# Reordering the first two groups of a fused cross-attention and expert kernel

## The chip, the cores and the metric

The kernel runs on one core of a Trainium2 chip. The metric is the device time of one execution, in microseconds (us). The engines are TensorE (PE, with its weight loads PEld), VectorE (DVE), ScalarE (ACT), GpSimd (POOL) and SyncE (SP), which issues most DMA transfers; ACT and POOL can issue transfers as well.

## The reference

One layer of a gated cross-attention block, with 16 sequences of 128 tokens and 256 channels, all in fp32. Cut to what matters:

```python
x = x + tanh(g_xattn) * attention(layernorm(x), ctx, mask, Wq, Wkv)   # 16 heads of 16 channels
x = x + tanh(g_ffn) * ffn(layernorm(x))                               # top 2 of 8 experts, and a shared FFN
# attention, per sequence:
q = layernorm(x) @ Wq.T;  k, v = split(ctx @ Wkv.T)                   # ctx: 128 rows of 192 channels
p = softmax(where(mask, (q * d ** -0.5) @ k.T, -1e9))                 # per head, over the 128 keys
out = p @ v
```

The change concerns the attention of the first four sequences alone.

## The kernel before

The 16 sequences are handled as 8 groups of two (256 tokens each). For each group g the kernel computes keys, queries and values on TensorE, the scores of each head, the softmax, the value product, the residual and the second norm, and then the router. The experts and the shared FFN follow after the groups.

**Per group.** For each half of the queries (j) and each half of the heads (h): `scores(g, j, h)` on PE (line 1422), `maxima(g, j, h)` on DVE (line 959), then per j `pieces` (line 965), a transpose `max_t` (line 1440 on PE, line 667 on ACT), the copy `max_rows`, `scores_t(g, j, h)` (line 1456), `exp` on ACT (line 673), the value product `values` (line 1473), a copy and a transpose (`heads_out`, `values_t`), and on DVE the division, the residual and the statistics of the second norm.

**Order.** Each engine runs one hand-written list, with semaphore waits. Behind an opening for groups 0 and 1 stands a loop over s from 2, which works on several groups at once: in step s the scores of group s-2, the queries of group s-1 and the keys of group s. The wait of an instruction holds everything behind it on its engine. The opening stands in the lists as follows.

- SP (line 406 on): loads of x in three parts (2, 2 and 12 blocks; the last is line 414, 1536 KB), context, weights; then the copies of group 0.
- POOL (line 561): powers for the first norm (`power1`), the memset of the ones rows, the third pieces of groups 0 and 1.
- ACT (line 722): `norm1(0)` (first norm of two blocks), `normed_t(0)` (its transpose out of PSUM), `norm1(1)`, and only then the pieces of group 0.
- DVE (line 1090): statistics and norms of blocks 0 to 3, the differences of group 0, statistics of the last 12 blocks (`stats(4, B)`, line 1101), the difference of group 1's keys, the last norms, four small conversions (line 1104).
- PE (line 1592): 56 warming products, the gates' product, 24 warming products, the transposes `normed_t(0)`, keys, queries, then group 1's keys and the values, `scores(0, 0, 0)`, `scores(0, 0, 1)`; the queries of group 1 open step s = 2 (line 1622), and `scores(1, 0, 0)` stands behind `scores_t(0, 0, 1)` (line 1666).

The functions that the diff touches:

## Time and profile before

| what | value |
|---|---|
| median of 3 runs | 333.09 us (332.68 to 334.06) |
| span of the profiled execution | 329.2 us |
| the profiled execution's own time | the profile gives its span alone; the median of the runs is 3.9 us above that |
| TensorE busy | 304.6 us (93%) |
| VectorE busy | 243.6 us (74%) |
| ScalarE busy | 169.2 us (51%) |
| GpSimd busy | 129.8 us (39%) |
| chain that ended last | PE 41%, DVE 18%, issue 17%, POOL 8%, DMA 7%, SP queue 5% |

The span runs from the first to the last instruction of the program. Busy shares are averages over stages that differ; the opening, the first 36 us or so, is a stage of its own, in which transfers are short of room and the engines wait for each other. The chain of waits is followed back from the last instruction, at each step to what released it. In a timeline row the columns are start, length, engine, line, operation, tile written and tiles read, shapes, count, and in brackets the idle time ahead of it and what ended it. SPq and ACTq are the issue of a transfer by that engine, not the transfer.

### The profile page before, as it was taken

Reading aid. Unit: us, or ns where it says so; the run is one execution under the profiler, and the core shown is the slowest. Engines: PE = TensorE matmul, PEld = TensorE weight load, DVE = VectorE, ACT = ScalarE, POOL = GpSimd, SP = SyncE. Lnnn points to the kernel's source line nnn. Section 1 sums busy time; section 2 is a strip of 40 time slices with the busy share of each in tenths; the row PEclk is TensorE's granted clock in tenths of the full one; section 3 lists DMA queues with packets and bytes.
Section 4 is the critical chain, followed back from the end, with each engine's and each line's share of the span. In section 5 each row is a group of like instructions: output and inputs, shape, how many; then the busy total and the mean of one; then the engine's idle time right before and its main releaser. Section 6 shows DMA issues by size and latency. Waiting matters only on the chain.

```text
span 329.2 us, 8082 instructions
## 1 busy us (share of the span) xinstructions
PE 304.6 (93%) x2505; PEld 244.5 (74%) x2505; DVE 243.6 (74%) x728; ACT 169.2 (51%) x322; POOL 129.8 (39%) x151
## 2 busy tenths in 40 slices
PE   7948889999989979998999989999999999999986
PEld 7627667787768755655465758889988898888875
DVE  4576597798999998687679976666666666633895
ACT  2444767777777744365495236444454444424131
POOL 5732143232465744506760085744333433331000
PEclk9998999999999999996999999999999999999999
DMA  7882776586666362166226112333333333103941
GB/s 232 255 217 80 227 197 207 161 263 193 189 186 177 123 178 84 50 201 250 98 98 164 44 34 83 106 94 108 94 103 98 97 85 111 64 16 133 416 153 64
DMA packets 34069, 47.18 MB, mean 143 GB/s; under 512 B 5519, under 2 KB 27667, under 8 KB 33522
## 3 DMA queue, kind: packets, MB, share of 16 engines
q1 hardware_dynamic: 28706, 34.61, 35.3%
q0 software_dynamic: 4320, 10.92, 9.9%
q10 hardware_dynamic: 1008, 1.18, 1.2%
q8 instruction: 22, 0.36, 0.5%
q14 instruction: 13, 0.11, 0.1%
HBM read 22.20 MB, written 12.62 MB: 106 GB/s over the span
## 4 chain that ended last, share of the span: by engine, by line
PE 41%; DVE 18%; issue 17%; POOL 8%; DMA 7%; SPq 5%; ACT 2%; POOLq 0%; DVEq 0%
PE ps L1744 27%; POOL dispatched L541 4%; DMA stacks<-work 4%; DVE x_all L1334 3%; DVE fc_lo L1177 3%; SPq L381 3%; PE ps L1790 3%; PE ps L1716 2%; PE ps L1562 2%; POOL rs L526 2%; PE ps L1437 1%; SPq L374 1%; DVE fc_lo L1183 1%; DMA stacks<-expert_rows 1%; PE ps L1407 1%
## 5 line engine op out<-in xcount | busy, mean ns | idle before, releaser
L597 POOL DMA_INDIRECT expert_rows<-v_s,slot_u x39 | 38.3, 982 | 58.6 <-ACT v_s L867 46.3
L963 DVE TENSOR_REDUCE mx<-ps 128x8 f32<-128x1024 f32 x32 | 39.1, 1223 | 13.0 <-PE ps L1437 12.7
L1284 DVE TENSOR_TENSOR act<-ps,sil 128x256 f32<-128x256 f32 x39 | 16.6, 425 | 29.9 <-ACT sil L860 29.8
L549 POOL TENSOR_TENSOR work<-work 128x512 bf16<-128x512 f32 x16 | 18.5, 1156 | 50.3 <-ACT work L646 50.2
L677 ACT ACTIVATE probs<-ps 128x1024 f32<-128x1024 f32 x32 | 32.7, 1022 | 9.4 <-PE ps L1470 9.4
L860 ACT ACTIVATE sil<-ps 128x256 f32<-128x256 f32 x39 | 15.0, 384 | 41.4 <-PE ps L1744 41.3
L1744 PE MATMUL ps<-fc_hi,xs_hi 128*128 x78 | 34.2, 439 | 1.4 <-DVE xs_lo L1265 1.4
L1744 PE MATMUL ps<-fc_hi,xs_lo 128*128 x78 | 30.7, 394 | 0.0
L1744 PE MATMUL ps<-fc_lo,xs_hi 128*128 x78 | 30.7, 394 | 0.0
L867 ACT ACTIVATE v_s<-ps,wt 128x256 f32<-128x256 f32 x39 | 18.5, 475 | 19.0 <-PE ps L1744 19.0
L1437 PE MATMUL ps<-stacks 96*128 96x128 bf16 x256 | 20.1, 222 | 7.0 <-DVE mx L963 3.3
L1437 PEld LDWEIGHTS ps<-stacks 96*128 96x128 bf16 x256 | 16.0, 100 | 10.3 <-DVE mx L963 4.8
L1744 PE MATMUL ps<-fc_hi,act_hi 128*128 x78 | 22.1, 283 | 0.2 <-DVE act_lo L1295 0.2
L1744 PE MATMUL ps<-fc_lo,act_hi 128*128 x78 | 22.0, 282 | 0.0
L1744 PE MATMUL ps<-fc_hi,act_lo 128*128 x78 | 21.9, 281 | 0.0
L1470 PEld LDWEIGHTS ps<-stacks 99*128 99x128 bf16 x256 | 15.8, 98 | 6.9 <-issue 5.4
L1470 PE MATMUL ps<-stacks 99*128 99x128 bf16 x256 | 19.7, 220 | 0.5 <-ACT probs L677 0.5
L1486 PE MATMUL ps<-probs,v_s 128*32 128x128 f32 x512 | 18.6, 281 | 1.1 <-DVE att L985 0.8
L1293 DVE CAST act_hi<-ps 128x256 fp32r<-128x256 f32 x39 | 16.5, 423 | 3.2 <-PE ps L1790 3.2
L541 POOL DMA_INDIRECT dispatched<-row_s,slot_u x16 | 16.0, 1000 | 7.4 <-issue 4.1
L1295 DVE TENSOR_TENSOR act_lo<-ps,act_hi 128x256 fp32r<-128x256 f32 x39 | 16.6, 424 | 1.3
L526 POOL TENSOR_TENSOR rs<-ve,mhalf 128x1 f32<-128x1 f32 x16 | 9.1, 566 | 21.4 <-DVE ve L996 21.4
(221 smaller groups left out, 828.4 us busy)
## 6 DMA issues: line engine op xcount, KB each, us to landing
stacks<-work SPq DMA_DIRECT2D x75, 128.0 KB, 3.1
xs_in<-dispatched SPq DMA_DIRECT2D x39, 129.0 KB, 2.0
fc_s<-in_fc SPq DMA_DIRECT2D x8, 512.0 KB, 5.2
stacks<-work POOLq DMA_DIRECT2D x18, 128.0 KB, 3.4
ctx_s<-in_ctx_t SPq DMA_DIRECT2D x8, 256.0 KB, 3.7
fc_s<-in_fc SPq DMA_DIRECT2D x8, 256.0 KB, 5.3
stacks<-expert_rows SPq DMA_DIRECT2D x2, 1024.0 KB, 5.8
probs<-expert_rows SPq DMA_DIRECT2D x2, 1024.0 KB, 9.9
```

Of the source, the lines that this page charges most:

```text
L541: nc.gpsimd.indirect_dma_start(xs, bass.IndirectOffsetOnAxis(slot_u[:, g, m:m + 1], 0), rows_of[g][:, m, :], None, bounds_check=NULL_ROW + ...
L549: nc.gpsimd.tensor_tensor(out[:, 2, :], rest, out[:, 1, :], ALU.subtract).then_inc(ready, 1)
L597: nc.gpsimd.indirect_dma_start(ys, bass.IndirectOffsetOnAxis(dst_u[:, r:r + 1], 0), y_out[:, r, :], None, bounds_check=2 * T - 1, oob_is_e ...
L677: nc.scalar.activation(probs[:, 2 * j + h], ps_t, ACT.Exp, scale=HD ** -0.5).then_inc(probs_ok[j][h], 1)
L867: nc.scalar.activation(y_out[:, r, :], ps[:, 5 + r % 2, 0:D], ACT.Copy, scale=wt[:, r:r + 1]).then_inc(y_ok, 1)
L963: nc.vector.reduce_max(mx[:, j, 8 * h:8 * h + 8], ps_s, AX_X).then_inc(max_ok[j][h], 1)
L1284: nc.vector.tensor_tensor(act[:, par], ps[:, 2 + par, FI:2 * FI], sil[:, par], ALU.mult).then_inc(act_ok, 1)
L1295: nc.vector.tensor_tensor(act_lo[:, par], whole, act_hi[:, par].bitcast(F32), ALU.subtract).then_inc(actt_ok, 1)
L1437: last = nc.tensor.matmul(ps_s[:, n, :], q_st[at], k_st[at], start=True, stop=True)
L1470: last = nc.tensor.matmul(ps_t[:, n, :], k_st[at], q_st[at], start=True, stop=True)
L1486: last = nc.tensor.matmul(ps_o[row:row + VW, blk:blk + P], v_s[:, g % 2, j, VW * head:VW * head + VW], probs[:, 2 * j + h, n, :], start=Tr ...
L1744: ins = nc.tensor.matmul(out, a, b, start=first and n == 0, stop=last and n == 2)
```

## The change

In words:

- PE computes the keys of group 0 ahead of the transposes of its rows, and runs 12 warming products behind the transposes instead of 24 ahead of them. The queries of group 1 move up between `scores(0, 0, 0)` and `scores(0, 0, 1)`. `scores(1, 0, 0)` stands ahead of `scores_t(0, 0, 1)`.
- ACT cuts the first key piece behind `norm1(0)`, the second one behind `normed_t(0)`, and only then runs `norm1(1)`. Its two copies of the first query piece are issued each behind a piece; the third copy goes to SP. The query pieces and the values of group 1 move up from step 3 to step 2, ahead of `norm1(2)`.
- DVE takes the key difference of group 0 ahead of the norm of blocks 2 and 3. The norm of the last 12 blocks and group 1's query difference stand between the first two maxima. The small conversions move to the end of step 2.
- POOL fills the ones rows behind the third pieces of group 0, with a wait on the third query piece instead of the one on the powers.
- SP issues the copies of group 1's first key piece ahead of the load of group 2's context, and group 1's query copies in step 2, with the row of maxima between the second and the third piece.

```diff
             stack_k(0, 0)
             stack_k(0, 1)
             stack_k(0, 2)
+            sp.wait_ge(q_ok[0], 1)
+            sp.dma_start(q_st[5:PIECES * HD:PIECES, 0].rearrange("p h t -> p (h t)"),
+                         q_pc[:, 0, :]).then_inc(qst[0], 16)
             stack_q(0, 1)
             stack_q(0, 2)
+            stack_k(1, 0)
 
             for s in range(2, G + 3):
-                if live(s - 3):
+                if live(s - 3) and s > 3:
                     max_rows(s - 3, 0)
-                if live(s - 2) and s > 2:
+                if live(s - 2) and s > 3:
                     stack_q(s - 2, 0)
                     stack_q(s - 2, 1)
                     stack_q(s - 2, 2)
...
                     load_shared(s - 3)
                 if live(s - 1):
                     stack_free(s - 1)
-                    stack_k(s - 1, 0)
+                    if s > 2:
+                        stack_k(s - 1, 0)
                     stack_k(s - 1, 1)
                     stack_k(s - 1, 2)
+                if s == 2:
+                    stack_q(1, 0)
+                    stack_q(1, 1)
+                    max_rows(0, 0)
+                    stack_q(1, 2)
 
             for e in range(EARLY, E):
                 load_first(e)
...
 
             power1(0, 2, 1)
             power1(2, 4, 2)
-            pool.wait_ge(rs1_ok, 2)
+            third(0, kst, k_rest, k_ok[1], k_pc, k_ok[2])
+            third(0, qst, q_rest, q_ok[1], q_pc, q_ok[2])
+            pool.wait_ge(q_ok[2], 1)
             nc.gpsimd.memset(k_f[PIECES * HD:PIECES * HD + 3, :], TWO_ONES).then_inc(kones_ok, 1)
             pool.wait_ge(kones_ok, 1)
-            third(0, kst, k_rest, k_ok[1], k_pc, k_ok[2])
-            third(0, qst, q_rest, q_ok[1], q_pc, q_ok[2])
             power1(4, B, 3)
             third(1, kst, k_rest, k_ok[1], k_pc, k_ok[2])
             third(1, qst, q_rest, q_ok[1], q_pc, q_ok[2])
...
 
             sa.wait_ge(gates_done, 1)
             nc.scalar.activation(tg[:, :], ps_c[:, 0:2], ACT.Tanh).then_inc(tanh_ok, 1)
+            def copy_of_q(row):
+
+                sa.wait_ge(q_ok[0], 1)
+                sa.dma_start(q_st[row:PIECES * HD:PIECES, 0].rearrange("p h t -> p (h t)"),
+                             q_pc[:, 0, :]).then_inc(qst[0], 16)
+
             norm1(0)
+            first(0, k_done, kst, k_pc, k_ok[0])
             normed_t(0)
+            second(0, kr_ok, k_rest, k_pc, k_ok[1])
             norm1(1)
-            first(0, k_done, kst, k_pc, k_ok[0])
-            second(0, kr_ok, k_rest, k_pc, k_ok[1])
             first(0, q_done, qst, q_pc, q_ok[0], ps_q0)
+            copy_of_q(0)
             second(0, qr_ok, q_rest, q_pc, q_ok[1])
-            sa.wait_ge(q_ok[0], 1)
-            for p, row in Q_ROWS:
-                if p == 0:
-                    sa.dma_start(q_st[row:PIECES * HD:PIECES, 0].rearrange("p h t -> p (h t)"),
-                                 q_pc[:, p, :]).then_inc(qst[0], 16)
+            copy_of_q(3)
             values_in(0)
             normed_t(1)
             for s in range(2, G + 2):
...
                     exp(s - 4, 1, 1)
                 if live(s - 5):
                     tokens_t(s - 5)
-                if live(s - 2) and s > 2:
+                if live(s - 2) and s > 3:
                     first(s - 2, q_done, qst, q_pc, q_ok[0])
                 if live(s - 3):
                     max_t(s - 3, 0)
-                if live(s - 2) and s > 2:
+                if live(s - 2) and s > 3:
                     values_in(s - 2)
                     second(s - 2, qr_ok, q_rest, q_pc, q_ok[1])
                 if live(s - 5):
...
                     max_t(s - 3, 1)
                 if live(s - 1):
                     first(s - 1, k_done, kst, k_pc, k_ok[0])
-                if s == 2:
-                    norm1(s)
                 if live(s - 3):
                     exp(s - 3, 0, 1)
                 if s == G + 1:
...
                     exp(s - 3, 1, 0)
                 if live(s - 1):
                     second(s - 1, kr_ok, k_rest, k_pc, k_ok[1])
+                if s == 2:
+                    first(1, q_done, qst, q_pc, q_ok[0])
+                    values_in(1)
+                    second(1, qr_ok, q_rest, q_pc, q_ok[1])
+                    norm1(s)
                 if live(s - 5):
                     second_score(s - 5)
                     second_row(s - 5, 1)
...
             first_norm(0, 2, 1)
             ve.wait_ge(x_in1, 16)
             stats(2, 4)
+            rest(0, ps_kq, k_ok[0], k_pc, k_ok[2], k_rest, kr_ok)
             first_norm(2, 4, 2)
-            rest(0, ps_kq, k_ok[0], k_pc, k_ok[2], k_rest, kr_ok)
             rest(0, ps_q0, q_ok[0], q_pc, q_ok[2], q_rest, qr_ok)
             ve.wait_ge(x_rest, 16)
             stats(4, B)
             rest(1, ps_kq, k_ok[0], k_pc, k_ok[2], k_rest, kr_ok)
-            first_norm(4, B, 3)
-            ve.wait_ge(const_ok, 11)
-            nc.vector.tensor_copy(e_f[:, :], e_i[:, :]).then_inc(dve_link, 1)
-            nc.vector.tensor_copy(t_f[:, :], t_i[:, :]).then_inc(dve_link, 1)
-            links[0] += 2
-            link(nc.vector.tensor_copy(dest_f[:, :], dest_i[:, :]))
-            link(nc.vector.tensor_scalar(er_f[:, :], e_f[:, :], float(R), None, ALU.mult))
+            def numbers():
+
+                ve.wait_ge(const_ok, 11)
+                nc.vector.tensor_copy(e_f[:, :], e_i[:, :]).then_inc(dve_link, 1)
+                nc.vector.tensor_copy(t_f[:, :], t_i[:, :]).then_inc(dve_link, 1)
+                links[0] += 2
+                link(nc.vector.tensor_copy(dest_f[:, :], dest_i[:, :]))
+                link(nc.vector.tensor_scalar(er_f[:, :], e_f[:, :], float(R), None, ALU.mult))
+
             relink()
             for s in range(2, G + 2):
                 if live(s - 2):
                     maxima(s - 2, 0, 0)
+                if s == 2:
+                    first_norm(4, B, 3)
+                    rest(1, ps_kq, q_ok[0], q_pc, q_ok[2], q_rest, qr_ok)
                 if live(s - 1) and s > 2:
                     rest(s - 1, ps_kq, k_ok[0], k_pc, k_ok[2], k_rest, kr_ok)
                 if live(s - 4):
...
                     residual(s - 3, 0)
                 if live(s - 2):
                     maxima(s - 2, 1, 0)
-                if live(s - 1):
+                if live(s - 1) and s > 2:
                     rest(s - 1, ps_kq, q_ok[0], q_pc, q_ok[2], q_rest, qr_ok)
                 if live(s - 5):
                     weights(s - 5)
...
                     logits(s - 4)
                 if live(s - 2):
                     pieces(s - 2, 1)
+                if s == 2:
+                    numbers()
                 if s == G + 1:
                     times_0(1)
                 if live(s - 4):
...
             pe.wait_ge(small_in, 32)
             pe.wait_ge(const_ok, 11)
             nc.tensor.matmul(ps_c[:, 0:2], ones_r[:, :], gate_r[:, :], start=True, stop=True).then_inc(gates_done, 1)
-            warm(24)
-            normed_t(0)
             keys_main(0)
             for c in range(2):
                 keys_rest(0, c)
+            normed_t(0)
+            warm(12)
             queries(0)
             keys_main(1)
             values_main(0)
...
             for j in range(2):
                 values_rest(1, j)
             scores(0, 0, 0)
+            queries(1)
             scores(0, 0, 1)
             for s in range(2, G + 2):
-                if live(s - 1):
+                if live(s - 1) and s > 2:
                     queries(s - 1)
                 if live(s - 2):
                     scores(s - 2, 1, 0)
...
                     for c in range(2):
                         keys_rest(s, c)
                         values_rest(s, c)
+                if s == 2:
+                    scores(1, 0, 0)
                 if s == G:
                     shared_0(2)
                     shared_0(3)
...
                     shared_0(10)
                 if live(s - 2):
                     scores_t(s - 2, 0, 1)
-                if live(s - 1):
+                if live(s - 1) and s > 2:
                     scores(s - 1, 0, 0)
                 if live(s - 4):
                     positions(s - 4)
```

## Rows read from the trace of the kernel before

**Rows 1.** Chain of waits, 0 to 80 us: start, length, what.

```profile
18.63 4.08 DMA stacks<-work
...
33.69 2.40 DMA stacks<-work
...
50.28 0.62 PE ps L1437 x8
```

**Rows 2.** Timeline of ACT, 6 to 50 us.

```profile
10.61 1.09 ACT L633 ACTIVATE work<-x_all,nm,rm 128x256 f32<-128x256 f32 x2 [0.85 <-DVE nm L936]
11.61 0.57 ACT L642 ACTIVATE work<-ps 128x512 bf16<-128x512 f32 x1
...
35.53 1.02 ACT L677 ACTIVATE probs<-ps 128x1024 f32<-128x1024 f32 x1
```

**Rows 3.** Timeline of PE, 6 to 42 us.

```profile
6.71 1.51 PE L1597 MATMUL ps<-ones_b 128*128 128x128 bf16 x24
...
9.92 1.13 PE L1378 MATMUL ps<-ctx_s,wk_s 64*128 64x256 f32 x4
...
22.75 0.62 PE L1437 MATMUL ps<-stacks 96*128 96x128 bf16 x8 [1.44 <-DMA stacks<-work]
24.69 1.03 PE L1437 MATMUL ps<-stacks 96*128 96x128 bf16 x8 [1.32 <-DVE mx L963]
25.52 3.12 PE L1407 MATMUL ps<-work,wq_s 128*128 128x256 f32 x8
...
30.41 0.62 PE L1437 MATMUL ps<-stacks 96*128 96x128 bf16 x8 [1.15 <-DVE mx L963]
...
34.87 0.62 PE L1470 MATMUL ps<-stacks 99*128 99x128 bf16 x8
36.13 0.62 PE L1437 MATMUL ps<-stacks 96*128 96x128 bf16 x8 [0.64 <-DMA stacks<-work]
36.69 1.08 PE L1486 MATMUL ps<-probs,v_s 128*32 128x128 f32 x32
...
39.89 1.95 PE L1407 MATMUL ps<-work,wq_s 128*128 128x256 f32 x8
```

**Rows 4.** Timeline of SP's transfer issues, 5 to 36 us.

```profile
5.19 0.48 SPq L414 DMA_DIRECT2D x_all<-in_x  x1
12.21 5.07 SPq L374 DMA_DIRECT2D stacks<-work  x6
...
30.48 3.81 SPq L381 DMA_DIRECT2D stacks<-work  x6
```

**Rows 5.** DMA issue at 5.1 to 5.2 us: KB, us from issue to landing.

```profile
x_all<-in_x SPq DMA_DIRECT2D x1, 1536.0 KB, 8.5
```

**Rows 6.** Busy time by stretch, then granted clock, DMA share, GB/s.

```profile
16.10:21.90 5.80, 2.84 (x12) 1.76 (x12) 4.03 (x22) 1.88 (x3) 2.54 (x2) 1.00 1.04 245
```

**Rows 7.** Timeline of DVE, 4 to 34 us.

```profile
14.69 4.01 DVE L924 BATCH_NORM_STATS2 st<-x_all 128x6 f32<-128x256 f32 x12
...
21.56 0.69 DVE L957 TENSOR_TENSOR work<-ps,work 128x512 f32<-128x512 f32 x1 [1.71 <-ACT work L642]
...
23.41 1.23 DVE L963 TENSOR_REDUCE mx<-ps 128x8 f32<-128x1024 f32 x1 [0.37 <-PE ps L1437]
...
27.51 0.17 DVE L971 TENSOR_SCALAR mx_pc<-mx 128x16 bf16<-128x16 f32 x1 [0.52 <-DVE mx L963]
```

**Rows 8.** Timeline of POOL, 9 to 28 us.

```profile
10.24 3.51 POOL L564 MEMSET stacks<- 3x4096 f32 x1
13.83 1.16 POOL L549 TENSOR_TENSOR work<-work 128x512 bf16<-128x512 f32 x1
...
19.93 2.27 POOL L522 TENSOR_TENSOR rs<-ve,mhalf 128x12 f32<-128x12 f32 x1 [3.26 <-DVE ve L931]
```

**Rows 9.** Busy time by stretch, then granted clock (third from the end), DMA share, GB/s.

```profile
24.50:27.90 3.40, 3.21 (x14) 2.76 (x15) 1.71 (x4) 0.00 (x0) 0.99 (x1) 0.50 0.46 126
...
150.80:157.60 6.80, 6.09 (x25) 3.11 (x26) 4.53 (x22) 3.65 (x7) 5.00 (x6) 0.50 0.51 195
```

## Prediction

> **What bounds the kernel now.** I read the chain of waits first, over the opening 80 us. It ties the opening to the copies that build the stacks: the last copy of group 0 is issued at 18.63 and takes 4.08 us, and the last one of group 1 ends just as TensorE begins that group's scores, at 36.13; group 2's begin at 50.28 [rows 1]. From 36.13 on the groups follow in steps of 14.15 us, each released by the one before, and the loads of later weights are issued inside these steps. What the opening gains or loses is therefore handed on to the end; nothing in the chain is held to a fixed time.
>
> The timelines of the engines come next, then the DMA issues. Group 0's first key copy is late for a reason of order: ScalarE normalizes group 1's rows (10.61, 1.09 us) before it cuts the first key piece at 11.61 [rows 2], although the key product ends at 11.05 and TensorE could have run it sooner: it stands behind the second warming series (6.71, 1.51 us) and the transposes [rows 3]. The load of the remaining rows of x, 1536 KB, is issued at 5.19 on SP and lands 8.5 us later, at 13.7 [rows 4, 5]. After that the DMA engines are far from full until 16.1, and then full to 21.9, at 245 GB/s [rows 6]. The hole between the two is what can be had.
>
> **The opening, part by part.** The key product goes ahead of the transposes and of 12 warming products, which replace 24; it needs only transfers that the wait for the gates outlasts. It starts at about 6.8, takes two halves of some 1.1 us [rows 3], and the piece (0.57) is cut by 9.6, ahead of the transposed rows and of group 1's normalization [rows 2]. SP then issues three copies from 9.6 instead of 12.21 [rows 4]. They gain less than these 2.6 us: on SP's queue they sit behind the 1536 KB, whose data end near 12.9, if landing takes the 0.8 us that lie between the end of the full stretch and the first scores (21.9 to 22.7) [rows 3, 5, 6]. The copy of the transposed rows follows the key piece, to 10.2, and the query product (1.95, [rows 3]) ends at 12.2.
>
> Query pieces: first 0.57, difference 0.69, second about 0.6, third 1.16 [rows 2, 7, 8]; with hops of 0.04 the third is ready at 15.4. The last copy is issued then, not at 18.63. ScalarE now issues two copies between its pieces instead of three behind them; at SP's price, 0.64 each (six in 3.81, [rows 4]), the second difference covers the first, and the values' product the other. The third is SP's own.
>
> **When are the twelve copies in?** Two sums. By data: 12 x 131 KB at 245 GB/s is 6.4 us after 12.9, and 0.8 to land: 20.1 [rows 6]. By issue: 15.4, 0.6 for the issue ahead of it, and the 4.08 us of [rows 1]: 20.1. Some loss between the queues added, I take 20.45 against 22.75: **-2.3**. The ends: if the data ran as fast as they could, group 1's first key difference on VectorE would hold the gain to about 3.0 (below). At the late end, SP's first six issues took 5.07 us instead of 3.8 [rows 4]; 1.2 more gives 21.5, a gain of 1.2.
>
> **The ones rows.** The memset (3.51 us, [rows 8]) moves behind both third pieces and a new wait on the query piece. Queued behind it on POOL are the power of the last twelve blocks and group 1's third pieces; VectorE's second norms wait for the power. The memset would run 15.4 to 18.9. The power needs the statistics of the rest of x, which now start at 14.69 and let the power go at 19.93, 5.2 us later [rows 7, 8]; started at 13.7 they end at 18.9. So the memset costs nothing; were this cover gone, each us past 18.9 would first use up the 1.2 us until VectorE asks for the power's result. The removed wait, on the first two powers, held nothing up. SP's new wait, on a piece whose successor it awaits next, costs its one copy.
>
> **Group 1, and what the new order makes wait.** Its first key piece must wait until all six key copies have landed, about 17.9 at the forecast's rate; the difference then waits for VectorE's statistics, to 18.9, and takes 0.69: 19.6, against 22.25 now [rows 7]. Group 1's query product now stands between the two halves of the first scores on TensorE, and its difference between the two maxima on VectorE. Added up from the start of the first scores: 0.5 of scores, 1.95 product, 0.57 piece, 0.69 difference, 1.23 maximum, 1.3 for the pieces of the maxima (idle 0.52, then 0.8 of four small instructions), 1.23 maximum, 0.25 of hops: 7.72 us to the start of scores (0,1,1). Before, it is 22.75 to 30.41, 7.66 [rows 2, 3, 7]. **+0.1**: the wait that VectorE gets is paid for by the product that no longer holds up the second block's scores.
>
> From there TensorE is nearly full in both. To the second half of group 0's transposed scores it is 30.41 to 34.87, 4.46. Before, group 1's scores follow, which wait for their copies, and the values from 36.69 to 37.77, in all 7.36. Now the scores of group 1 come first: 4.46 + 0.56 + 0.62 + exponential 1.02 + half the values 0.54 + hops 0.15 = 7.35 [rows 2, 3]. **0.0**: the stall on the copies goes, and the exponential that was hidden in it comes out. Group 1's query copies: five issues of 0.64 from about 24, the row of maxima, then the last one at about 28 [rows 4]; with the 2.40 us of [rows 1] it lands near 30.4, and TensorE asks at 32.6. The row of maxima is wanted by 29.8 and issued at about 27; its way to landing shows in no row, so between nothing and a full copy's 2.40 of delay, and as it is much smaller than a copy I take no delay. VectorE's four small conversions (0.5) move into its idle time behind the second pieces; group 2's context is loaded behind three more issues, 1.9 us, and is wanted some 4 us after it lands.
>
> Sum: -2.3 + 0.1 + 0.0 = **-2.2 us** at an equal clock.
>
> **The clock.** TensorE's granted clock is half from 24.5 to 27.9 [rows 9]. It fell after TensorE had paused twice, 1.44 and 1.32 us, for the copies and for a maximum, with 0.62 of work between. The query product in that stretch took 3.12 instead of 1.95 [rows 3]: +1.17, which lies within the 7.66. The new order has a thin stretch too, 23.5 to 28.2, with two groups of scores in it, so a half stretch probably comes behind it, over work that TensorE does without a pause. Bounds: 0, if it ends as the full work begins; 1.7, half of its 3.4 us. I take the middle, **+0.85**.
>
> The Trainium skill, TensorE: Matmul & The Clock Gate, Part 1, calls half the clock the idle state, brought back by an idle stretch and lifted by activity; read so, the pauses here, some 2 us at most, would not bring it back, and the sum would be -2.2. The trace disagrees: the clock fell after pauses of 1.44 and 1.32 us.
>
> **Time.** The profiled execution has a span of 329.2; the median of the runs, 333.09, is 3.9 above it, which I take as what lies around the span, unchanged. -2.2 + 0.85 is -1.35: 331.7. A measurement of this kernel tells about 0.5% from no change, 1.7 us, so faster begins under 331.4.
>
> **Rivals.** One: no half stretch hits full work. For it: the new opening leaves TensorE fewer long pauses before 23. Against: [rows 9]. It gives -2.2: 330.9. It is also what the page's rule gives.
>
> Two: the copies come little earlier, because SP or the queue is late, -1.2 in place of -2.3. For it: SP's slow issues [rows 4], and key copies that wait behind x whenever they are issued [rows 5]. Against: the hole before 16.1. -1.2 + 0.1 + 0.85: 332.8.
>
> Three, the slower side: two half stretches. The first is brought by the pause before the first scores (19 to 20.4) and hits group 1's query product as it does today, +1.17; the second hits the full work, +1.7. It decides once the two cost over 2.2 together: -2.2 + 2.87 = +0.67, 333.8. For it: from 150.8 to 157.6 the clock stays at half for 6.8 us on end [rows 9]. Against: the steps from 36.13 on show none.
>
> **Chances.** Forecast 0.50 (its own range 330.9 to 332.6), one 0.24, two 0.14, three 0.12. Under 331.4 lie one's 0.24, two fifths of the forecast, 0.20, and 0.02 of two: faster 0.46. Over 334.8 lie the upper tail of three, 0.05, and 0.06 for a wait that I have not seen: slower 0.11. The rest, 0.43, is the same. The range takes in the early end of the copies without a half stretch (-2.9: 330.2), rival two and most of three: 330.2 to 333.6.
>
> **What would show it.** First key copy issued near 9.6 and landed after 14; scores of group 0 at 20.0 to 21.0; the power right behind the memset near 18.9; group 1's query product between the first two groups of scores; scores (0,1,1) near 28.2; scores of group 1 near 32.6, not released by a DMA; steps of 14.15 us afterwards. The forecast is wrong if the copies land past 21.5, if TensorE waits for group 1's copies with the transposed scores queued behind, if the power starts past 20, or if the lead at group 2's scores is gone by the end.

## Result and profile after

The changed kernel takes 335.39 us (median of 20 runs, 333.38 to 339.10), the kernel before 333.84 (20 runs, 330.64 to 335.31): a ratio of 1.0059, 95% interval 1.0036 to 1.0082. It is slower by about 2 us, 0.6%, by the ratio (1.6 us by the medians), where 1.4 us less had been forecast. A second set gave 1.0050 (1.0017 to 1.0082). A ratio leaves out runs over 1.5% above the fastest of their kernel; where a kernel's runs spread with the granted clock, ratio and medians can differ, so below the medians of all runs stand first.

The profile shown of the changed kernel is of its fastest run, 333.38 us, with a span of 331.6. So 1.8 us lie around the span, here and, within 0.1, in every run of these two kernels that lists both. The prediction had taken 3.9.

ScalarE of the changed kernel, timeline (against [rows 2]); then its transfer issues on SP ([rows 4]), and the load of x ([rows 5]):

```profile
9.12 0.60 ACT L652 ACTIVATE work<-ps 128x512 bf16<-128x512 f32 x1 [0.72 <-PE ps L1401]
...
12.39 0.60 ACT L652 ACTIVATE work<-ps 128x512 bf16<-128x512 f32 x1 [0.30 <-PE ps L1430]
```

```profile
9.74 3.89 SPq L374 DMA_DIRECT2D stacks<-work  x6
13.68 0.60 SPq L419 DMA_DIRECT2D stacks<-work  x1
14.40 2.45 SPq L381 DMA_DIRECT2D stacks<-work  x3
...
24.25 3.20 SPq L381 DMA_DIRECT2D stacks<-work  x5
28.16 0.84 SPq L403 DMA_DIRECT2D stacks<-mx_t  x1
```

```profile
x_all<-in_x SPq DMA_DIRECT2D x1, 1536.0 KB, 9.7
```

The first pieces come as worked out: keys at 9.12, queries at 12.39, first key copy issued at 9.74. But x now takes 9.7 us to land instead of 8.5. The chain of waits has group 0's last copy ([rows 1]) issued at 15.64, three us earlier than before, and longer on its way:

```profile
15.64 5.47 DMA stacks<-work
```

VectorE and GpSimd, timelines ([rows 7, 8]):

```profile
14.93 4.02 DVE L940 BATCH_NORM_STATS2 st<-x_all 128x6 f32<-128x256 f32 x12 [1.22 <-DMA x_all<-in_x]
...
22.95 0.71 DVE L951 TENSOR_TENSOR rm<-rs,mask_f 128x12 f32<-128x12 f32 x1
...
26.15 0.69 DVE L987 TENSOR_SCALAR mx_pc<-mx 128x16 bf16<-128x16 f32 x1
```

```profile
15.66 3.51 POOL L576 MEMSET stacks<- 3x4096 f32 x1
20.24 2.27 POOL L532 TENSOR_TENSOR rs<-ve,mhalf 128x12 f32<-128x12 f32 x1 [1.08 <-DVE ve L947]
22.48 1.15 POOL L559 TENSOR_TENSOR work<-work 128x512 bf16<-128x512 f32 x1
25.65 1.15 POOL L559 TENSOR_TENSOR work<-work 128x512 bf16<-128x512 f32 x1 [2.02 <-ACT work L656]
```

The statistics start 1.2 us later than forecast (14.93, not 13.7), by as much as x lands later, and the power waits for them, not for the memset. TensorE ([rows 3]):

```profile
21.15 0.62 PE L1460 MATMUL ps<-stacks 96*128 96x128 bf16 x8 [1.67 <-DMA stacks<-work]
21.61 1.95 PE L1430 MATMUL ps<-work,wq_s 128*128 128x256 f32 x8
23.39 0.61 PE L1460 MATMUL ps<-stacks 96*128 96x128 bf16 x8
26.10 1.00 PE L1460 MATMUL ps<-stacks 96*128 96x128 bf16 x8 [2.10 <-DVE mx L979]
...
28.66 1.03 PE L1460 MATMUL ps<-stacks 96*128 96x128 bf16 x8 [0.84 <-DVE mx L979]
29.49 1.06 PE L1441 MATMUL ps<-ident,work 128*128 128x128 f32 x4
30.35 1.91 PE L1396 MATMUL ps<-ctx_s,wk_s 128*128 128x256 f32 x4
...
35.20 0.62 PE L1460 MATMUL ps<-stacks 96*128 96x128 bf16 x8
35.66 0.61 PE L1493 MATMUL ps<-stacks 99*128 99x128 bf16 x8
36.20 0.64 PE L1509 MATMUL ps<-probs,v_s 128*32 128x128 f32 x16
37.39 0.65 PE L1509 MATMUL ps<-probs,v_s 128*32 128x128 f32 x16 [0.54 <-ACT probs L687]
```

The first scores start 1.60 us earlier (21.15 against 22.75), scores (0,1,1) 1.75 earlier (28.66 against 30.41), and group 1's scores (35.20) no longer wait for a copy. Then the lead goes: 0.93 is left at group 1's scores, behind work at half clock, the second half of the values waits 0.54 for an exponential, and group 2's scores start at 50.47, 0.18 later than before. Group 7's first ones are 1.66 later (126.8 before). Twice in the opening a small VectorE instruction takes 0.7 us instead of 0.17, until GpSimd's third piece beside it ends (26.15 + 0.69 and 25.65 + 1.15).

Three stretches (clock third from the end):

```profile
18.70:36.90 18.20, 13.12 (x106) 10.03 (x104) 11.48 (x35) 8.34 (x15) 5.01 (x4) 0.81 0.43 114
116.00:136.00 20.00, 17.25 (x179) 11.31 (x177) 17.80 (x50) 9.72 (x17) 7.96 (x10) 1.00 0.37 108
150.00:162.00 12.00, 10.12 (x64) 5.92 (x63) 7.91 (x32) 4.88 (x9) 8.14 (x9) 0.72 0.56 205
```

Every clock record is at one of the two levels, full or half, so the time at half in a stretch is twice its length times what the mean lacks to 1: here 6.9 us in the opening, where the profile before has 3.4 [rows 9], none about 120, 6.7 about 152 in both.

### The profile page after: what moved, and what is told of

Read it like the earlier page. It is cut to its first block, busy times and chain, and to the rows that moved or that the text cites. A ratio compares the mean times of both kernels' runs of the same rounds, so it can differ in the third digit from the quotient of the medians.

```text
span 331.6 us, 8058 instructions
## 1 busy us (share of the span) xinstructions
PE 306.0 (92%) x2493; PEld 245.4 (74%) x2493; DVE 245.3 (74%) x728; ACT 169.5 (51%) x322; POOL 129.8 (39%) x151
## 4 chain that ended last, share of the span: by engine, by line
PE 45%; DVE 18%; issue 17%; POOL 9%; DMA 6%; ACT 2%; SPq 2%; POOLq 0%; DVEq 0%
PE ps L1770 27%; POOL dispatched L551 4%; DMA stacks<-work 3%; DVE x_all L1357 3%; DVE fc_lo L1200 3%; PE ps L1816 3%; PE ps L1742 2%; PE ps L1620 2%; PE ps L1430 2%; PE ps L1585 2%; SPq L381 2%; POOL work L559 2%; DMA stacks<-expert_rows 1%; POOL rs L536 1%; PE ps L1460 1%
## 5 line engine op out<-in xcount | busy, mean ns | idle before, releaser
L1770 PE MATMUL ps<-fc_hi,act_hi 128*128 x78 | 22.3, 286 | 0.2 <-DVE act_lo L1318 0.2
L1493 PE MATMUL ps<-stacks 99*128 99x128 bf16 x256 | 20.1, 222 | 0.5 <-ACT probs L687 0.5
```

The lines of the kernel that those rows point to most:

```text
L1493: last = nc.tensor.matmul(ps_t[:, n, :], k_st[at], q_st[at], start=True, stop=True)
L1770: ins = nc.tensor.matmul(out, a, b, start=first and n == 0, stop=last and n == 2)
```

## Experiments

A table further on brings the profiles together. Where an expectation speaks of group 0's values product at 38.2 us, the mark is the scores right behind it, (1,0,1). "Warming products" are more of the 128x128 products that the kernel begins with, into a bank that nobody reads at that time; they change no result.

**1. The clock of the opening.** Both kernels get warming products in front of the waits at which TensorE paused:

```diff
+            def fill(count):
+                for n in range(count):
+                    nc.tensor.matmul(ps[:, 4, 0:P], ones_b[:, :], ones_b[:, :], start=True, stop=True)
...
+            fill(22)
             scores(0, 0, 0)
```

(a_fill: 14, 8, 22, 34 and 14 of them, ahead of `normed_t(1)`, `values_main(1)`, `scores(0,0,0)`, `scores(0,1,0)` and `scores(0,1,1)`; b_fill: 26, 8, 22, 18, 14, the fourth ahead of `scores(0,0,1)`.)

> Fills TensorE's pauses of the opening in the changed kernel with warming products into a free bank (14, 8, 22, 34, 14 of them), so that the clock has no reason to fall before 33 us. Clock theory (the change wins 1.6 us at the first scores and loses more to a longer half stretch): 1.0 to 2.5 us under the kernel before, 3 to 4 under the changed one, granted clock 0.98 or more. Order theory (group 1's queries between the first scores, and its scores ahead of the transposed ones, cost the time): still 0.5 to 2 us over the kernel before. Theory of a loss further down: lead of 1.5 us or more at group 2's scores in the trace, but not at the end of the span.

> The same filling of the pauses in the kernel before (26, 8, 22, 18, 14 products). Clock theory: about 1.2 us under the kernel before, the price of the one half stretch there, and 1 to 2 us slower than the changed kernel with its pauses filled. Order theory: also about 1.2 under, but faster than the changed kernel filled.

Measured: a_fill 333.49 us (12 runs), ratio 1.0032 (0.9991 to 1.0073); b_fill 332.96 (12 runs), 0.9989 (0.9958 to 1.0019); the kernel before on the same chip 333.95. Neither profile falls to half before 119 us. So the opening's falls come from the pauses, and filling them takes 1.9 us off the changed kernel's median (335.39 in the first set) and 1.0 off the one before. a_fill's median is 0.5 below the kernel before, where the clock theory had 1.0 to 2.5 below and the order theory 0.5 to 2 above: neither range is met. With the opening's clock equal the changed order is not the faster one. a_fill leads at the first scores by 1.4 us, and has 0.69 left at group 1's second scores, where b_fill is 1.12 ahead of the profile before without any earlier copy.

**2. Parts of the change, without warming products.** g0_only keeps group 0's part (keys first, memset and copies moved) and puts group 1's queries, rests and scores back; s100_back is the changed kernel with one line moved:

```diff
-                if s == 2:
-                    scores(1, 0, 0)
...
                 if live(s - 2):
                     scores_t(s - 2, 0, 1)
-                if live(s - 1) and s > 2:
+                if live(s - 1):
                     scores(s - 1, 0, 0)
```

> The part of the change for group 0 alone (keys first, ones rows behind the pieces, copies behind their pieces); group 1's queries, copies, norms and scores stand where they stood. Clock theory: first scores at 21.1 as with the whole change, half the loss of clock, time within 1 us of the kernel before. Order theory: 1.0 to 1.6 us under the kernel before, since the lead of the copies stays and nothing is interleaved.

> The changed kernel with group 1's first scores back behind the second half of group 0's transposed scores. Clock theory: within 0.4 us of the changed kernel (335.4 beside 333.8 of the kernel before). Order theory: 0.6 to 1.0 us faster than the changed kernel, since the exponential no longer comes out from under those scores.

Measured: g0_only 334.23 us (12 runs), ratio 1.0023 (0.9992 to 1.0053); s100_back 335.57 (12 runs), 1.0058 (1.0018 to 1.0098). g0_only starts the first scores 0.95 earlier (at 21.80, not the 21.1 expected) and has nothing of it left at 28.5 us; it is within 1 us of the kernel before, as the clock theory had it. s100_back is as slow as the changed kernel (335.39, and 335.09 in experiment 5), again as the clock theory had it: in the kernel as it runs, putting the line back gains nothing that shows. Its profile does not tell why, since it runs 13.7 us of the opening at half clock (21.05 to 34.70), which only g1_only's (experiment 6) has as well. Parts must be compared at an equal clock.

**3. The same parts with warming products.**

> Only group 0's part of the change, with warming products in TensorE's pauses up to the first block's scores, so that the clock is equal to that of the filled kernel before (332.96 us). Theory A (with the clock equal, group 0's part gains its lead, and group 1's part gives it back): first scores 0.9 to 1.6 us earlier than before's 22.75, no half clock up to 40 us, a lead of 1.5 to 2.5 us still there at the scores of group 2 (50 us; the filled kernel before had 1.7, the filled changed kernel 1.3), median 331.8 to 332.4, 0.6 to 1.2 below the filled kernel before. Rival B (any lead of the opening is lost in the waits of the loop): lead at group 2 no more than the 1.7 of the filled kernel before, median 332.7 to 333.3.

> Only group 1's part of the change (its query product between the first scores, scores(1,0,0) ahead of the transposed ones, its copies and rests moved) on before's opening, with warming products in the pauses. Theory A: first scores as in the filled kernel before (22.6), no half clock up to 40 us, but the lead at group 2's scores 0.5 to 1.2 us smaller than the 1.7 of the filled kernel before, median 333.4 to 334.0. Rival B: as the filled kernel before, 332.7 to 333.3. Rival C (group 1's part gains and it was group 0's that cost): lead at group 2 above 2 us, median under 332.5.

> The filled changed kernel (333.49 us) with scores(1,0,0) back behind the transposed scores; everything else of the change stays. Theory A1 (scores(1,0,0) ahead of them uncovers the exponentials of block (0,0), which cost the filled changed kernel 1.2 us between 36.1 and 38.2): the shift at group 0's values product (38.2) returns from -0.69 to -1.5 to -1.9, median 332.3 to 332.9. Rival A2 (the wait moves to scores(1,0,0), which then starts later and holds up group 1's chain by as much): shift at 50 us as in the filled changed kernel (-1.3), median 333.2 to 333.7.

Measured: g0_fill 333.69 us, ratio 1.0028 (0.9995 to 1.0061); g1_fill 333.78, 1.0003 (0.9973 to 1.0034); a_fill_s100 332.27, 1.0022 (0.9980 to 1.0065); 12 runs each, the kernel before 333.46. By their profiles, all at full clock up to 87 us, group 2's scores stand against 50.28 at: b_fill -1.72, g0_fill -1.41, g1_fill +0.37, a_fill -1.30, a_fill_s100 -2.31.

- Group 0's part alone gains nothing (-1.41 against -1.72; 0.9 us of lead at the first scores): theory A's first half falls. GpSimd, TensorE and VectorE show why, in g0_fill's timelines:

```profile
20.30 2.27 POOL L525 TENSOR_TENSOR rs<-ve,mhalf 128x12 f32<-128x12 f32 x1 [0.78 <-DVE ve L937]
```

```profile
21.65 0.62 PE L1447 MATMUL ps<-stacks 96*128 96x128 bf16 x8
```

```profile
22.61 0.17 DVE L941 TENSOR_TENSOR rm<-rs,mask_f 128x12 f32<-128x12 f32 x1 [1.86 <-POOL rs L525]
...
23.63 1.23 DVE L969 TENSOR_REDUCE mx<-ps 128x8 f32<-128x1024 f32 x1 [0.21 <-DVE er_f L1116]
```

The first scores are there at 22.3, but VectorE stands in the second norms, 1.86 us, for the power, which starts no earlier than before (20.30; 19.93 in [rows 8]) as it waits for the statistics of x; four conversions follow, and only then the maximum. Group 1's part puts the norms behind that maximum. The lead then gets as far as scores (0,0,1), where a_fill is 1.15 us ahead of b_fill; at scores (0,1,1) 0.22 of it is left (experiment 4).
- Group 1's part alone costs 2.1 us at group 2 (+0.37 against -1.72), more than theory A's 0.5 to 1.2. Of this, 1.0 us goes between the first scores and scores (0,1,1), where its query product stands (from -0.09 to -0.25, while b_fill goes from -0.17 to -1.30), and 1.2 us between group 1's first and second scores (from -0.90 to +0.29), as in a_fill (from -1.89 to -0.69).
- Scores (1,0,0) back behind the transposed scores gives 1.0 us back in the profiles (-2.31 against -1.30): theory A1. The medians (332.27 against 333.49) do not show it: they come from two sets, and a_fill_s100's holds runs at a clock of 0.99 and more; at 0.983 to 0.985 its median is 333.58, a_fill's 333.04. Both parts without that line lead the filled kernel before by 0.6 at group 2, in the profiles.

**4. Full clock all the way.** The three kernels b_fill, a_fill and a_fill_s100 also get warming products at five later places, in pauses that take 0.4 to 1.4 us in the profile before, ahead of where most profiles fall (the expectation counts six):

```diff
+                    if s == G:
+                        pe.wait_ge(o_read[0], G - 2)
+                        fill(12)
                     max_t(s - 2, 0)
...
+                if s == G:
+                    pe.wait_ge(v_ok, G)
+                    fill(24, 6)
                 if live(s - 3):
                     values_t(s - 3, 1)
...
+            pe.wait_ge(max_ok[1][1], G)
+            fill(14, 0)
             values(g, 1, 0)
...
+            fill(12, 0)
             values_t(g, 1)
...
+            fill(16, 0)
             tokens_t(g)
```

(the second argument is the bank; the added waits keep the products off banks still being read)

> The kernel before with warming products in TensorE's pauses of the opening (as in the filled kernel before, 332.96 us) and in six later pauses of 0.6 to 1.4 us around 116, 120, 148, 151 and 156 us, ahead of the places at which half-clock stretches came at 120 to 127 and 152 to 158 us in nearly all profiles. Theory K (the clock falls behind these pauses cost 2 to 3 us each): mean granted clock 0.99 or more, median 329.0 to 331.0. Rival (the falls come for another reason, or the products hold up what follows): a half stretch still shows at 120 or 152, median 332.5 or more.

> The changed kernel with the same warming products, opening and later pauses: both kernels at full clock nearly all the way, so what is left between them is the order alone. Theory A (the order with scores(1,0,0) ahead is no gain at equal clock, since it gives 1.2 us back at group 0's exponentials): median 0.2 to 0.8 above the kernel before with the same products (329.4 to 331.6). Rival B (at equal clock the changed order gains what was forecast, 1 to 2 us, and its loss was the clock alone): 1 us or more below it.

> The same with scores(1,0,0) back behind the transposed scores. Theory A: it keeps the 2.3 us of lead at group 2's scores, gives up 0.6 to 1.3 of it in the loop's own waits, and ends 0.4 to 1.2 us below the kernel before with the same products: 328.0 to 330.2, faster than both kernels of the case by 1 % or more. Rival B: no different from the other two, within 0.3 us of the kernel before with the same products.

| kernel | median of 6 runs (mean) | ratio to the kernel before, 333.47 us |
|---|---|---|
| b_all, the order before | 328.24 us (328.58) | 0.9865 (0.9826 to 0.9904) |
| a_all, the changed order | 329.25 us (328.77) | 0.9868 (0.9828 to 0.9909) |
| as_all, scores (1,0,0) back | 327.72 us (327.85) | 0.9844 (0.9807 to 0.9882) |

Theory K holds: 17 of the 18 runs are at a clock of 0.999 or 1.000, and the medians are 4.2 to 5.8 us below the kernel before, b_all's below the range that K gave. Between the orders six runs each do not decide: the changed one is 0.2 us slower than the one before by the means (1.0 by the medians), the one with scores (1,0,0) put back 0.7 faster (0.5), and by the runs' own spread a difference of two means is uncertain by some 1.0 to 1.2 us. So as_all's theory A, 0.4 to 1.2 below b_all, is not told apart from its rival by the times. Rival B of a_all, a gain of 1 to 2 us at equal clock, lies at the very edge of that and has the profiles against it: a_all's span is 0.64 longer than b_all's, as_all's 0.88 shorter, and in both pairs of profiles (a_fill and b_fill, a_all and b_all) the lead goes at the same places. as_all beats both kernels of the case, almost all of it by the clock.

Where the lead goes at full clock, TensorE's timelines of b_all and then a_all show:

```profile
22.56 0.62 PE L1437 MATMUL ps<-stacks 96*128 96x128 bf16 x8
...
29.06 0.62 PE L1437 MATMUL ps<-stacks 96*128 96x128 bf16 x8
...
35.11 0.62 PE L1437 MATMUL ps<-stacks 96*128 96x128 bf16 x8 [0.95 <-DMA stacks<-work]
```

```profile
21.36 0.62 PE L1460 MATMUL ps<-stacks 96*128 96x128 bf16 x8 [0.28 <-DMA stacks<-work]
21.82 1.95 PE L1430 MATMUL ps<-work,wq_s 128*128 128x256 f32 x8
...
28.87 0.62 PE L1460 MATMUL ps<-stacks 96*128 96x128 bf16 x8
```

The first scores are 1.20 us earlier. From there to scores (0,1,1) the order before takes 6.50 us and the changed one, with group 1's query product and difference between the two maxima, 7.51: 0.19 is left. Then the wait for group 1's copies (0.95) goes, and an exponential comes out. Where that line costs, TensorE's timelines of a_all and as_all show:

```profile
31.48 0.62 PE L1493 MATMUL ps<-stacks 99*128 99x128 bf16 x8 [0.68 <-DMA stacks<-mx_t]
...
34.18 0.62 PE L1460 MATMUL ps<-stacks 96*128 96x128 bf16 x8
34.64 0.61 PE L1493 MATMUL ps<-stacks 99*128 99x128 bf16 x8
35.18 0.65 PE L1509 MATMUL ps<-probs,v_s 128*32 128x128 f32 x16
36.36 0.64 PE L1509 MATMUL ps<-probs,v_s 128*32 128x128 f32 x16 [0.54 <-ACT probs L687]
```

```profile
33.92 0.62 PE L1493 MATMUL ps<-stacks 99*128 99x128 bf16 x8
34.37 0.61 PE L1460 MATMUL ps<-stacks 96*128 96x128 bf16 x8
34.92 1.38 PE L1509 MATMUL ps<-probs,v_s 128*32 128x128 f32 x32
```

In a_all the second transposed scores stand behind scores (1,0,0), so their exponential starts 0.72 us later, at 35.29 instead of 34.57, and the values stop for it; the values end at 37.00 and 36.30. The 0.68 ahead of the first row is another wait, new in both: the row of maxima sits on SP behind five query copies of group 1. Their issue takes 4.62 us in a_all:

```profile
24.43 4.62 SPq L381 DMA_DIRECT2D stacks<-work  x5
29.09 0.84 SPq L403 DMA_DIRECT2D stacks<-mx_t  x1
```

**5. Is the half clock the kernels' own?**

> The changed kernel as it is, beside the others on one chip and for a second profile. Theory K (most of its loss is the clock: the profile shown was its fastest of 20 runs, and the others granted 0.005 to 0.01 less): median 335.0 to 335.7, and a profile above 334 us that shows more than the two stretches of half clock (26.2 to 33.0 and 152.5 to 159.3), the added ones in the opening (before 40 us) or near 120 us, where four of four experiments fell. Rival (the order alone costs it): a second profile with the same two stretches and a span of 333 or more.

> The kernel before, a second profile. Theory K1 (its opening falls to half clock for one stretch, and the changed kernel's for two): half clock in the opening for 3.4 us, starting at 24 to 28 us, as in the profile shown; the rest of its loss of clock near 120 and 152 us. Rival K2 (the single stretch of the profile shown was chance): 6.8 us or more at half in the opening.

> The kernel before, a third profile, with the same expectations: K1 has 3.4 us at half clock in the opening, K2 6.8 us or more.

> The changed kernel, a third profile. K1: 6.8 us at half clock in the opening, starting at 26 to 27 us, as in its two profiles so far, with scores(1,0,0) ahead leaving TensorE's values product of group 0 (38.2 us in the profile before) 0.3 to 0.8 us later than in the profile shown of the kernel before. K2: 3.4 us or 10 us, at another place.

> The changed kernel, a fourth profile. Its three so far were of runs at 332.75 to 334.2 us, below its median of 335.4, and the kernel before's second and third profiles have 10.24 us at half clock in the opening, where its loss is small (0.95 to 1.20 us at group 2's scores). Theory P (with as many half stretches the changed kernel loses more, since they lie on fuller work): a run of 335 us or more with 6 half stretches in all, 2 or 3 of them in the opening, and the shift at 126.8 us 3 us or more. Rival Q (the typical run has more half clock in the opening, as the kernel with scores(1,0,0) back had, 13.65 us): 4 half stretches in the opening and 2 us or more of shift at group 2's scores.

> The changed kernel, a fifth profile, with the same expectations: P has 2 or 3 half stretches in the opening and 3 or more behind it, Q 4 in the opening.

> The changed kernel, a sixth profile, with the same expectations: P has 2 or 3 half stretches in the opening and 3 or more behind it, Q 4 in the opening.

after_again: 335.09 us (12 runs), ratio 1.0050 (1.0017 to 1.0082), and in its profile half clock near 122 us too, as its theory K had it. The other six are one profiled run each. Mean granted clock by stretch (windows as above), and TensorE's starts against the profile before:

| profiled run | us | 18.7 to 36.9 | 116 to 136 | 150 to 162 | group 2's scores (50.28) | first scores of group 7 (126.8) |
|---|---|---|---|---|---|---|
| before | 331.0 (span + 1.8) | 0.91 | 1.00 | 0.72 | 0 | 0 |
| before_2 | 333.86 | 0.72 | 0.91 | 0.72 | +1.20 | +2.64 |
| before_3 | 333.83 | 0.72 | 0.91 | 0.86 | +0.95 | +3.77 |
| after | 333.38 | 0.81 | 1.00 | 0.72 | +0.18 | +1.66 |
| after_again | 334.19 | 0.81 | 0.91 | 0.72 | +0.71 | +2.75 |
| after_3 | 332.75 | 0.72 | 1.00 | 0.72 | +0.58 | +1.49 |
| after_4 | 334.72 | 0.81 | 0.83 | 0.86 | +1.04 | +4.66 |
| after_5 | 333.29 | 0.81 | 1.00 | 0.72 | +0.21 | +1.50 |
| after_6 | 334.85 | 0.81 | 0.91 | 0.72 | +1.09 | +3.20 |

Two rows of before_2 behind it:

```profile
18.70:36.90 18.20, 14.97 (x86) 10.85 (x86) 9.65 (x33) 8.13 (x16) 4.58 (x3) 0.72 0.50 126
116.00:136.00 20.00, 18.02 (x176) 12.47 (x175) 16.52 (x44) 9.23 (x17) 8.81 (x11) 0.91 0.37 108
```

K1 falls: the single half stretch (3.4 us at half clock) in the opening of the profile before was luck. The second and third profiles of that kernel have 10.2 us at half there, the changed kernel 6.8 in five of six. Q falls too: none of these six has 13.7. P is shown in part. A stretch of 3.4 us at half costs differently by place: each of the two more in before_2's and before_3's openings 0.5 us at group 2's scores ((1.20 + 0.95) / 2, by two); one near 122 us some 1.4 to 1.7 (before_2 from +1.21 to +2.64 between 119.5 and 126.8, after_6 from +1.55 to +3.20); two there 2.9 (after_4, +1.80 to +4.66). No profile of a run of the changed kernel over 335 us was caught. The runs of all sets that list a clock, by its mean (20 of 130 lie outside these rows):

| mean granted clock | before: runs, median | changed: runs, median |
|---|---|---|
| 0.966 to 0.971 | 44, 334.00 us | 17, 336.15 us |
| 0.972 to 0.976 | 21, 333.15 us | 14, 334.70 us |
| 0.977 to 0.982 | 11, 332.17 us | 3, 333.29 us |
| 0.994 to 1.000 (b_all, a_all) | 6, 328.24 us | 6, 329.25 us |

So the changed kernel does not lose by more half clock: the mean over all runs is 0.9727 before and 0.9715 after, a quarter of a us at the 2 us or so that 0.01 costs. It loses at the same clock, and the more the lower; at full clock its loss, 1.0 by the medians and 0.2 by the means, is not clear of noise.

**6. Group 1's part alone, as it runs.**

> Only group 1's part of the change on before's opening, without warming products. Theory A (scores(1,0,0) ahead uncovers the exponentials, and the half clock lies on the full work behind it): first scores at 22.7 to 22.8, values product of group 0 0.8 to 2.0 us later than before, median 335.0 to 337.0. Rival (only both parts together cost anything): 333.5 to 334.3, as before.

Measured: 335.40 us (median of 8 runs, 328.82 to 337.14), the kernel before 333.52. The spread is the clock again: 0.990 at 328.82, 0.964 at 337.14. The ratio, 0.9876 (0.9826 to 0.9926), counts only the three runs at a clock of 0.979 and more. So median and ratio differ in sign, and neither is a verdict on the order; at one clock, 0.964, it takes 336.19 to 337.14 where the kernel before takes 334.72 to 335.99. Its profile is of the run at 337.14:

```profile
22.75 1.03 PE L1454 MATMUL ps<-stacks 96*128 96x128 bf16 x8
23.58 3.43 PE L1424 MATMUL ps<-work,wq_s 128*128 128x256 f32 x8
26.85 0.61 PE L1454 MATMUL ps<-stacks 96*128 96x128 bf16 x8
```

Here the half clock (19.75 to 26.6) meets the query product between the two first scores: 3.43 us instead of 1.95, and scores (0,0,1) start 2.16 later than before, with the same first scores. In the profile before, a query product at half clock (3.12, [rows 3]) lay behind both and held up less. Theory A had the values 0.8 to 2.0 us later; at their mark they are 3.9 later, with 13.7 us at half clock in this opening. Its median, 335 to 337, is met, but through the clock of these eight runs.

## Why the prediction was wrong

The steps that failed are the three terms of the sum. -2.2 us was called a gain at an equal clock, but the stretch of 7.66 us that the changed order was measured against held a half stretch. Between the kernels that run at full clock there is no gain left at group 1's second scores (from the shifts of TensorE's starts, us):

| term of the sum | forecast | a_fill against b_fill | a_all against b_all | as_all (the line back) against b_all |
|---|---|---|---|---|
| copies: to the first scores | -2.3 | -1.25 | -1.20 | -1.33 |
| query product: from there to scores (0,1,1) | +0.1 | +1.03 | +1.01 | +1.02 |
| scores (1,0,0) ahead: from there to (1,0,1) | 0.0 | +0.65 | +0.45 | -0.14 |
| sum | -2.2 | +0.43 | +0.26 | -0.45 |

As it runs the changed kernel loses 1.1 to 2.2 us at one clock (experiment 5); what that has beyond these terms is open.

- **Copies, -2.3: right in kind, too large.** The issues came within 0.3 us of the sum (third query piece ready at 15.6, forecast 15.4), but they did not set the landing. In after_6 the last copy is issued at 17.25 and takes 3.96, here at 15.64 and takes 5.47: both land at 21.1 to 21.2. The sum by data is the one that holds, with another start: x landed at 14.9, so its data end at 14.1 and not 12.9, and 6.4 + 0.8 more is 21.3, the start of the scores (21.15). What was left out is that x itself lands later when the copies are issued earlier (last section), and that 8.5 us was the shortest landing of seven. Measured against the profile before -1.60, and -1.1 to -1.6 in the other profiles with both parts; at full clock the size is rival two's -1.2.
- **The memset for nothing: right.** It ran from 15.66 to 19.17 and the power waited for the statistics; these ended at 20.1 and not 18.9, by x.
- **Query product between the first scores, +0.1: wrong by 0.9.** The changed kernel's own stretch was worked out well: 7.51 us against the forecast 7.72. What it was set against was not: 7.66 holds the half stretch, which the prediction itself prices at 1.17 there, and at full clock the order before takes 6.50. So the wait that VectorE gets is not paid for. At half clock it costs more: after_3 goes from a lead of 1.44 us at the first scores to 0.40 at the second, and group 1's part alone loses 2.16.
- **Scores (1,0,0) ahead, 0.0: wrong by some 0.5.** The exponential that comes out was seen and priced, but against a stall of the profile before that could be had back otherwise: with the line where it was and the earlier copies, as_all has neither that stall nor that wait. At full clock the line costs 0.7 to 1.0 us at group 1 in the profiles; the times do not show it. And the row of maxima was taken at no delay within bounds of 0 to 2.40; it waits 0.54 to 0.68 in as_all and a_all behind the five copies. In the span that was to be 7.35, a_all takes 8.13 (28.87 to 37.00).
- **The clock, +0.85: wrong in kind.** A profile of one run was taken as the kernel's state. Two of three profiles of before have three half stretches in the opening, not one, so the sum started from a run that was 2.8 us better than the median (331.0 against 333.84); this was hidden by setting 3.9 us around the span where 1.8 lie. The extra half stretch that was charged to the change is not the change's: in the later profiles the opening of either kernel has two or three. What the change does is to lay work without slack where they fall.
- **The lead is handed on to the end: not contradicted.** Against the profile before, as_all keeps 2.06 at group 2's scores and 0.99 at 88 us, as a VectorE instruction hit by GpSimd's third piece takes 1.1 us of it (below). But b_all loses as much there, from 1.63 to 0.47: the profile before was spared. Against b_all, as_all's lead is 0.43 at group 2's scores and 0.51 at 88 us.
- **Rivals.** Three had the sign and a mechanism that was seen (half clock on group 1's query product), and under half the size, +0.67; it was given 0.12. One, no half stretch on full work, is what the warming products of the opening make: a_fill is then 1.30 us ahead of the profile before at group 2's scores, not 2.2, and not ahead of b_fill. The Trainium skill, TensorE: Matmul & The Clock Gate, Part 1, was set against the row there: it says that idle time brings the half clock and that activity lifts it. The runs agree with it in so far as products in pauses of 0.4 to 2.1 us kept the clock full (b_all, a_all, as_all). The prediction read it to mean that such pauses are too short to bring the half clock; the runs contradict that.
- **Chances.** Slower by over 0.5% had 0.11. The range's upper end, 333.6, lies under the kernel before's own median of 20 runs.

**Shown** by the profiles, in two pairs at full clock: the copies gain 1.2 us, the query product takes 1.0 of it, and scores (1,0,0) ahead more than the rest; group 0's part is worth nothing without group 1's. Shown by the times: at full clock the three orders lie within 1.6 us, all 4 to 6 us faster. **Open:** which order is the fastest at full clock, by the times; and where a run at 336 us loses its last us: the places of the half stretches (P) fit, but no such run was profiled, and at low clock putting the line back (s100_back) gained nothing.

## What to carry over

Profile a kernel several times before reading its clock: one run had a third of the half-clock time that the opening usually has, and the base of the sum was 2.8 us off. A term that is a difference needs both its sides at the same clock: +0.1 became +1.0 when the order before was measured at full clock too. Compare two orders at an equal clock (here by warming products in the pauses), then the parts of a change separate; and a pause in TensorE is worth filling for its own sake before its order is improved. When a product is moved ahead of another, follow who feeds from the one that now comes second, at the new rate and not at the old stall.

## Not expected

- With the copies issued earlier, the load of x ahead of them lands later: with group 0's part in, x takes 8.9 to 10.4 us (mean 9.7, 13 profiles), without it 8.5 to 9.7 (mean 9.0, 7 profiles). That the copies behind it are the cause was not tested by itself.
- Several small VectorE instructions lasted until the GpSimd instruction beside them ended. as_all, VectorE and then GpSimd:

```profile
81.38 1.07 DVE L1082 TENSOR_TENSOR cum<-cum,new 128x8 bf16<-128x8 bf16 x1
```

```profile
81.27 1.16 POOL L559 TENSOR_TENSOR work<-work 128x512 bf16<-128x512 f32 x1 [2.72 <-ACT work L656]
```

Both end at 82.4; in the profile before the same instruction took 0.17 (at 83.27, just ahead of the third piece), and a maximum that reads PSUM beside the piece kept its 1.2. In b_all and a_all the instruction took 1.16 and 1.07. The Trainium skill, Trainium Architecture — The Big Picture, What this means for kernel authors, says that VectorE and GpSimd contend for a shared port by an exclusive lock; these rows agree.
- Warming products in the pauses were worth more than all the reordering, 5 us against 1.6 between the best and the worst order at full clock; 17 of the 18 runs with all of them lost next to no clock.
